# Second half of the heads weighed with high and low halves, in a fused cross-attention and mixture-of-experts kernel

## The reference

```
x = x + tanh(g_xattn) * xattn(layernorm(x), ctx)       # q @ Wq, ctx @ Wk, ctx @ Wv, softmax, @ Wo + bo
x = x + tanh(g_ffn) * (sum over 8 of 32 experts, weighted, + shared expert)(layernorm(x))
```

## Time and profile before

| | us |
|---|---|
| median of 3 runs | 660.29 (659.31 to 665.08) |
| profiled execution | 661.07 |
| its span | 658.9 |
| attention loop, 24 batches | about 61 to 310 |
| expert stage | from about 350 |

### The profile page before, as it was taken

How to read it: one execution, slowest core, us unless ns; L and a number is a source line. 1 busy time by engine, 2 the same in 40 slices (tenths; PEclk the granted TensorE clock), 3 DMA queues, 4 the chain that set the end, 5 groups by cost and what they waited for, 6 DMA issues and landing times.

```text
span 658.9 us, 13957 instructions
## 1 busy us (share of the span) xinstructions
PE 642.4 (97%) x3716; PEld 482.5 (73%) x3716; DVE 540.0 (82%) x1379; ACT 389.6 (59%) x738; POOL 344.7 (52%) x364
## 2 busy tenths in 40 slices
PE   8999999999999999999999999999999999999997
PEld 5666765767667676676658878788887878788785
DVE  6979978899898998989887969878695877869565
ACT  3565665666666665666556555555555555555553
POOL 4224645464544645546302656666565656657653
PEclk9999998999999999999999999999999999999999
DMA  8323222233323332223225844263645435364550
GB/s 185 101 65 82 80 71 61 79 78 79 80 63 80 80 78 80 62 84 84 59 68 142 184 109 129 73 163 81 163 113 128 131 73 140 86 159 113 139 137 16
DMA packets 63276, 65.58 MB, mean 100 GB/s; under 512 B 26112, under 2 KB 41600, under 8 KB 63232
## 3 DMA queue, kind: packets, MB, share of 16 engines
q1 hardware_dynamic: 63232, 65.07, 39.3%
HBM read 61.64 MB, written 2.88 MB: 98 GB/s over the span
## 4 chain that ended last, share of the span: by engine, by line
PE 68%; issue 9%; DVE 6%; ACT 5%; DMA 4%; POOL 4%; SPq 2%; DVEq 1%; ACTq 0%; POOLq 0%
PE bank L1220 13%; PE bank L1221 13%; PE bank L1222 13%; PE bank L1309 7%; PE bank L1333 5%; POOL halves L538 4%; DVE halves L820 3%; PE bank L1256 3%; PE bank L1276 3%; DMA sums<-wbc 2%; PE bank L1285 2%; PE bank L1279 2%; PE bank L1282 2%; DMA sums<-area 1%; SPq L311 1%
## 5 line engine op out<-in xcount | busy, mean ns | idle before, releaser
L538 POOL TENSOR_TENSOR halves<-area,halves 128x512 fp32r<-128x512 f32 x134 | 174.4, 1301 | 139.5 <-ACT halves L687 135.9
L700 ACT ACTIVATE area<-bank 128x512 f32<-128x512 f32 x136 | 81.4, 599 | 111.8 <-PE bank L1222 108.8
L625 ACT ACTIVATE area<-bank 128x512 f32<-128x512 f32 x128 | 69.5, 595 | 104.1 <-PE bank L1285 104.1
L1176 DVE TENSOR_TENSOR bank<-area,bank 128x512 f32<-128x512 f32 x128 | 88.7, 693 | 50.5 <-PE bank L1222 50.1
L1220 PE MATMUL bank<-x2t_hi,w_hi 128*128 128x512 f32 x272 | 110.3, 406 | 0.1
L1221 PE MATMUL bank<-x2t_hi,w_lo 128*128 128x512 f32 x272 | 107.2, 394 | 0.0
L1222 PE MATMUL bank<-x2t_lo,w_hi 128*128 128x512 f32 x272 | 106.4, 391 | 0.0
L472 POOL TENSOR_TENSOR ctx_hi<-ctx_raw,ones_col 128x128 fp32r<-128x128 f32 x32 | 27.4, 858 | 137.7 <-DMA ctx_raw<-ctx_t 137.7
L687 ACT ACTIVATE halves<-area 128x512 fp32r<-128x512 f32 x136 | 85.0, 626 | 17.1 <-DVE area L1187 16.7
L829 DVE TENSOR_REDUCE row_max<-bank 128x4 f32<-128x512 f32 x128 | 82.1, 684 | 6.1 <-PE bank L1256 3.4
L1187 DVE TENSOR_TENSOR area<-bank,wbc 128x512 f32<-128x512 f32 x128 | 86.5, 681 | 0.5 <-DMA wbc<-rows_dram 0.5
(11 more groups left out here) (149 smaller groups left out, 1261.7 us busy)
## 6 DMA issues: line engine op xcount, KB each, us to landing
wbc<-rows_dram SPq DMA_DIRECT2D x126, 256.0 KB, 4.2
inverse_bc<-inverse_dram SPq DMA_DIRECT2D x64, 256.0 KB, 3.5
w_raw<-experts SPq DMA_DIRECT2D x32, 102.0 KB, 2.0
ctx_raw<-ctx_t SPq DMA_DIRECT2D x32, 64.0 KB, 1.9
ctx_keys<-ctx_nat SPq DMA_DIRECT2D x32, 64.0 KB, 2.0
out<-area SPq DMA_DIRECT2D x7, 256.0 KB, 3.9
max_rows<-max_t SPq DMA_DIRECT2D x64, 4.0 KB
area<-wq_t SPq DMA_DIRECT2D x1, 512.0 KB, 4.7
```

What stands on the lines that cost most here:

```text
L538: nc.gpsimd.tensor_tensor(hid_lo[:, u % SLOTS, :], hid[:, u % HIDS, :], raw(hid_hi[:, u % SLOTS, :]), ALU.subtract).then_inc(hidlo_ready, 1)
L700: nc.scalar.activation(silu_g[:, u % 2, :], gate_ps[u % 2][:], ACT.Silu).then_inc(silu_ready, 1)
L1176: nc.vector.tensor_tensor(up_ps[u % UPS][:], silu_g[:, u % 2, :], up_ps[u % UPS][:], ALU.mult)\
```

## The change

From batch t = 3 on (LATE_FROM), and up to t = 27, the second half of the heads is weighed with halves too. `late_high` on ScalarE rounds the exponentials of groups 2 and 3 into the same `p_hi[q]` that the first half uses, once the first half's weighing has let it go. `late_low` on GpSimd makes the low halves, at the start of the next batch in its queue. `weigh_late` on TensorE takes the place of `weigh` for t - 1. As the buffers are shared, `probs_high` now waits for the late weighing of the batch before. Keys are split from t = 3 on.

Moved: `g_low` in odd b goes ahead of both scalings; `u_out(t, 0, 0)` goes behind `g_high` and `late_high`; `probs_high` always behind the two `u_out` of t - 1; `load_raw` on SyncE ahead of the maxima and the sums.

```diff
--- before.py
+++ after.py
@@ -68,7 +68,7 @@
 LN_AT = {0: range(0, 8), 1: range(8, RSTD_LEVELS)}
 AHEAD = 2
 STATS_AT = {2: (2,), 3: (3,), 4: (4,), 5: (5,), 6: (6, 7)}
-HALVED_FROM = CB
+HALVED_FROM, LATE_FROM = CB, CB - 1
 NB_SEAM = (NCH - 2) * CB
 SEAM = {4: (1, 6), 5: (6, 10), 6: (10, 14), 7: (14, 21)}
 LATE = {NB - 2: 3, NB - 1: 12}
@@ -208,6 +208,7 @@
         maxt_done, maxt_ready = sem("maxt_done"), sem("maxt_ready")
         st_done, exp_ready = sem("st_done"), sem("exp_ready")
         phi_ready, plo_ready = sem("phi_ready"), sem("plo_ready")
+        latehi_ready, latelo_ready = sem("latehi_ready"), sem("latelo_ready")
         keyshi_ready, keyslo_ready = sem("keyshi_ready"), sem("keyslo_ready")
         u_done, u_ready, inverse_ready = sem("u_done"), sem("u_ready"), sem("inverse_ready")
         norm_ready = [sem("norm_even_ready"), sem("norm_odd_ready")]
@@ -358,13 +359,13 @@
             def attention(c, first, last):
                 for b in range(CB):
                     t = CB * c + b
+                    if not last:
+                        wait_first(ctx_ready, t + 1)
+                        load_raw(b, (t + CB) * P)
                     if not (last and b == CB - 1):
                         load_max_row(t + 1, (b + 1) % 2, t - 1)
                     if not (first and b == 0):
                         spread_sums(t - 1, (b - 1) % CB)
-                    if not last:
-                        wait_first(ctx_ready, t + 1)
-                        load_raw(b, (t + CB) * P)
                     if not (last and b >= 2):
                         wait_first(wsplit_ready, t + 1)
                         load_weights(b % 2, (t + 2) * WSTEP)
@@ -481,9 +482,16 @@
                 wait(pool, u_done, 4 * (t - 2) + 4)
                 nc.gpsimd.tensor_tensor(keys_hi[:, b % 2, :], ctx_keys[:, b, :], ones_col[:].broadcast_to([P, 3 * CD]),
                                         ALU.mult).then_inc(keyshi_ready, 1)
-                pool.wait_ge(keyshi_ready, t + 1 - HALVED_FROM)
+                pool.wait_ge(keyshi_ready, t + 1 - LATE_FROM)
                 nc.gpsimd.tensor_tensor(keys_lo[:, b % 2, :], ctx_keys[:, b, :], raw(keys_hi[:, b % 2, :]), ALU.subtract)\
                     .then_inc(keyslo_ready, 1)
+
+            def late_low(t):
+
+                for q in range(2):
+                    pool.wait_ge(latehi_ready, 2 * (t - LATE_FROM) + q + 1)
+                    nc.gpsimd.tensor_tensor(p_lo[q], probs_t[:, 2 + q, :, :].rearrange("p h n -> p (h n)"),
+                                            raw(p_hi[q]), ALU.subtract).then_inc(latelo_ready, 1)
 
             def split_weights(slot, t, nth, contexts):
 
@@ -517,7 +525,9 @@
             def attention(c, first, last):
                 for b in range(CB):
                     t = CB * c + b
-                    if not first and not last:
+                    if not first and not (last and b > 0):
+                        late_low(t - 1)
+                    if not last and not (first and b < CB - 1):
                         split_keys(b, t, c)
                     split_weights(b % 2, t, 2 * c + b // 2, NB if last else t + CB)
                     add_bias(t, c)
@@ -628,10 +638,17 @@
             def probs_high(t):
 
                 act.wait_ge(exp_ready, 4 * t + 2)
-                wait(act, u_done, 4 * t - 2)
                 for q in range(2):
+                    act.wait_ge(u_done, 4 * (t - 1) + q + 3)
                     nc.scalar.activation(p_hi[q], probs_t[:, q, :, :].rearrange("p h n -> p (h n)"), ACT.Copy)\
                         .then_inc(phi_ready, 1)
+
+            def late_high(t, q):
+
+                act.wait_ge(exp_ready, 4 * t + q + 3)
+                act.wait_ge(u_done, 4 * t + q + 1)
+                nc.scalar.activation(p_hi[q], probs_t[:, 2 + q, :, :].rearrange("p h n -> p (h n)"), ACT.Copy)\
+                    .then_inc(latehi_ready, 1)
 
             def attention(c, first, last):
                 for b in range(CB):
@@ -641,15 +658,13 @@
                     exp_of(t, 0, 1)
                     if not (last and b == CB - 1):
                         max_out(t + 1, (b + 1) % 2, 2 * c + (b - 1) // 2 + 1)
-                    if not first and not last and b % 2 == 1:
+                    if not (first and b == 0):
+                        for q in range(2):
+                            u_out(t - 1, (b - 1) % CB, 1, q)
+                    if not first and not last:
                         probs_high(t)
                         if b == 1:
                             xt_high(c + 1)
-                    if not (first and b == 0):
-                        for q in range(2):
-                            u_out(t - 1, (b - 1) % CB, 1, q)
-                    if not first and not last and b % 2 == 0:
-                        probs_high(t)
                     if last and b == CB - 1:
                         x2t_out(1, scores_ps[1])
                     if first and b == 1:
@@ -661,9 +676,17 @@
                     exp_of(t, 1, 1)
                     if last and b == 1:
                         sigmoid_high(0, ut_ps)
+                    late = not last and not (first and b < CB - 1)
+                    if late:
+                        late_high(t, 0)
+                    if late and b % 2 == 1:
+                        g_high(2 * c + 2 + b // 2, b // 2)
+                        late_high(t, 1)
                     u_out(t, b, 0, 0)
-                    if b % 2 == 1 and not last:
-                        g_high(2 * c + 2 + b // 2, b // 2)
+                    if late and b % 2 == 0:
+                        late_high(t, 1)
+                    if first and b == 1:
+                        g_high(2, 0)
                     u_out(t, b, 0, 1)
                     if last and b == 0:
                         x2t_out(0, ut_ps)
@@ -834,7 +857,6 @@
 
                 for q in range(2):
                     dve.wait_ge(phi_ready, 2 * (t - HALVED_FROM) + q + 1)
-                    wait(dve, u_done, 4 * (t - 1) + q + 1)
                     nc.vector.tensor_tensor(p_lo[q], probs_t[:, q, :, :].rearrange("p h n -> p (h n)"),
                                             raw(p_hi[q]), ALU.subtract).then_inc(plo_ready, 1)
 
@@ -1050,6 +1072,8 @@
 
                         if h == 0 and not first:
                             batch_stats(t - CB, b)
+                        if h == 1 and b % 2 == 1 and first:
+                            g_low(2 * c + 2 + b // 2, b // 2)
                         if h == 1:
                             if first and b >= 2:
                                 normalise(t - 2, (b - 2) % CB, 0)
@@ -1062,8 +1086,6 @@
                         if first:
                             for n in STATS_AT.get(step_of_chunk, ()):
                                 chunk_stats(n)
-                        if h == 1 and b % 2 == 1 and first:
-                            g_low(2 * c + 2 + b // 2, b // 2)
                         if h == 1:
                             if not (first and b < 3):
                                 residual(t - 3)
@@ -1111,10 +1133,10 @@
                     batch_mean(t - CB, b)
                     if b == CB - 1:
                         keep_means(t - b - CB)
-                    normalise(t - 2, (b - 2) % CB, 0)
                     if b % 2 == 1:
                         g_low(2 * c + 2 + b // 2, b // 2)
-                    normalise(t - 2, (b - 2) % CB, 1)
+                    for q in range(2):
+                        normalise(t - 2, (b - 2) % CB, q)
 
             attention(0, True, False)
             with dve.Fori(1, NCH - 1) as c:
@@ -1288,7 +1310,7 @@
             def weigh_halves(t, b, q):
 
                 if q == 0:
-                    pe.wait_ge(keyslo_ready, t + 1 - HALVED_FROM)
+                    pe.wait_ge(keyslo_ready, t + 1 - LATE_FROM)
                 pe.wait_ge(phi_ready, 2 * (t - HALVED_FROM) + q + 1)
                 wait(pe, u_ready, 4 * (t - 1) + q + 3)
                 cols = slice(0, CD + 1) if q == 0 else slice(CD, 3 * CD)
@@ -1297,6 +1319,21 @@
                 nc.tensor.matmul(ps, keys_lo[:, b % 2, cols], p_hi[q], start=False, stop=False)
                 pe.wait_ge(plo_ready, 2 * (t - HALVED_FROM) + q + 1)
                 nc.tensor.matmul(ps, keys_hi[:, b % 2, cols], p_lo[q], start=False, stop=True).then_inc(u_done, 1)
+
+            def weigh_late(t, b):
+
+                pe.wait_ge(keyslo_ready, t + 1 - LATE_FROM)
+                cols = (slice(0, CD + 1), slice(CD, 3 * CD))
+                ps = (u_ps[0][0:CD + 1, :], u_ps[1][0:P, :])
+                for q in range(2):
+                    pe.wait_ge(latehi_ready, 2 * (t - LATE_FROM) + q + 1)
+                    pe.wait_ge(u_ready, 4 * t + q + 1)
+                    nc.tensor.matmul(ps[q], keys_hi[:, b % 2, cols[q]], p_hi[q], start=True, stop=False)
+                    nc.tensor.matmul(ps[q], keys_lo[:, b % 2, cols[q]], p_hi[q], start=False, stop=False)
+                for q in range(2):
```

(7 more changed lines are left out.)

## The result

| | before | after |
|---|---|---|
| median of 6 runs, us | 660.4 (659.3 to 665.1) | 691.9 (689.8 to 694.6) |
| ratio | | 1.046, 95% interval 1.043 to 1.050 |
| profiled execution, us | 661.1 | 693.7 |
| its span, us | 658.9 | 691.9 |
| loop, from the `scores` of batch 4 to those of batch 28, us | 61.00 to 309.89 = 248.9 | 60.82 to 340.00 = 279.2 |

The time is 0.9 us above the range of the forecast (657 to 691) and 12 above its point. The direction was right. Most of the loss is in the loop: +30.3 us of the +33.0 in the span.

What follows compares the result with a forecast made beforehand. TensorE was taken as the bound, VectorE close behind. Per pair −0.4 work, −0.3 wait, +0.75 and +1.65 gave +1.7 us; twelve pairs, 20.4 us, on 661.07 gave 681.5, as median 680.7, rounded to 680; range 657 to 691.

Steps and rivals of the forecast that it cites:

- The mechanism that made the forecast slower: VectorE's two-SBUF-input scalings and GpSimd's SBUF-reading subtractions exclude each other, so project_out waits; a pair gets 1.7 us longer.
- its two waits: TensorE at project_out waits 0.75 us in one tile of a pair and 1.65 us in the other.
- the wait for L820: TensorE's 0.3 us wait before the even tile's scores, for the queries' low halves, goes: 3.6 us saved over 12 pairs.
- TensorE's own work: Weighing two heads' groups with halves instead of fp32 saves 0.2 us a tile over 25 tiles, 5 us.
- the order in chunk 0 and the last chunk: Edits at the loop's two ends touch one tile each and cost under 1 us.
- Odd into even tile: From the even tile's scores, two scalings and one subtraction last 3.55 us; project_out, reached at +2.75, waits 0.75.
- The even tile: Two scalings and two subtractions meet from about +8.6, 4.7 us until +13.35; project_out, reached at +11.7, waits 1.65.
- The rest of the pair: After the second project_out starts, 9.1 us less the 0.3 us wait, 8.8, giving a pair of 22.15 us.
- SyncE's queue: With load_raw ahead, scaling's end to invert takes 5.65 us instead of 5.5; closes on 22.2 us a pair, late next.
- rival 3: SyncE's queue sets the pace as scaling delays return through inverse, maxima and sums: pairs 22.6 to 23.0, 687 to 692; 0.08.
- its only gain: Moving load_raw ahead ends the context's split at +7.4 to +7.9, out of the way of scalings and subtractions; no price.
- Rival 1: Subtractions early enough or running beside the scalings, so project_out finds its operands at +2.75: only savings stay, 652.5 us; 0.17.

Runs made afterwards that it cites:

- experiment 3: Changed kernel with both loop scalings replaced by a sum with one input in SBUF, scaling by inverse sums left out: 661.0 us, ratio 0.998 to the kernel before.
- 7b: Kernel before with only the low halves of the queries moved ahead of both scalings: 657.8 us, ratio 0.994.
- experiment 2: Changed kernel with each GpSimd subtraction replaced by two 16-column subtractions and two 496-column fills, similar time, almost no SBUF reading: 680.7 us, ratio 1.029.

## Why the prediction was right in direction and too small

The mechanism that made the forecast slower is the one that the runs show, and its two waits came out to 0.3 us. What failed is a step beside it, and terms put at nothing. In its own terms the forecast was +20.4 us; the span grew by 33.0. (The sum of 680.7 us also rounds to 681, not to 680.) Of the 12.6 between them 4.2 are in pairs at full clock (mainly the wait for L820, taken as gone), 5.7 in the long pairs of the loop (the clock, which has no term, and the first pair) and 2.7 outside the loop.

**TensorE's own work.** 0.2 us a tile. In the run of experiment 3, where nothing else interferes, scores to project_out fall from 2.96 to 2.67 (−0.29), but the stretch behind project_out grows from 2.38 to 2.45, twice a pair. A pair goes from 20.5 to 20.24: 0.13 us a tile, 3 us in all instead of 5. And that is eaten by the two ends of the loop.

**The two ends.** The prediction has "the order in chunk 0 and the last chunk" at under 1 us. The first pair is 24.59 in the run of experiment 3 against 20.55 before: the transpose of the maxima waits for VectorE's residual there, in the changed kernel's timeline of TensorE as in that run. Behind the loop TensorE waits for VectorE's normalised x, and the tile there is 2.5 us longer than before; in the kernel before that product has no such wait (L820 in this row is a line of after.py and not the L820 of the prediction):

```profile
64.41 0.38 PE L1288 MATMUL bank<-ident,row_max 128*16 128x128 f32 x1 [2.40 <-DVE x_sb L883]
...
349.56 0.66 PE L1249 MATMUL bank<-ident,xn 128*128 128x128 f32 x4 [1.60 <-DVE xn L820]
```

**The wait for L820.** Wrong, and this is the step of the sum whose mechanism failed: "L820 now starts when ScalarE's high halves come ... TensorE's 0.3 us wait goes: 12 pairs × 0.3 = 3.6 us". The stretch at whose end it lies did not shrink: 6.48 and 6.77 us instead of 6.36 and 6.75. VectorE works in order, and invert, ahead of it, waits 1.08 us for the sums in the pairs b = 2 and 3; I had priced load_raw's 0.6 us in that very queue and not carried it over. The saving was also too large by its own rows: L820's end moves from 166.43 to 166.25, which is 0.2 us and not 0.3. 7b, which has the move without load_raw's, shows it at 3.7 us in the median, with a clock that did not fall in its profiled execution.

**Odd into even tile.** Scalings and one subtraction in 3.55 us, project_out from +2.75 to +3.5. Measured 3.45, and +3.42 in the median. Right.

**The even tile.** Scores at +5.9 (measured +5.86), late_high(E, 0) ready at +8.7 (+8.7: the subtraction starts at 188.15, +8.8), invert at +9.15 (+8.85), four operations ending at +13.35 (+13.43), project_out there (+13.5). Right to 0.3 us, and experiment 3 shows the cause.

**The rest of the pair.** 8.8 us, from project_out of O to the next pair. Measured 8.9 and 9.2 in pairs at full clock (2.45 + 6.48 and 2.45 + 6.77): the 0.3 of L820 and 0.07. This is the pair of 22.55 instead of 22.15, some 4 to 5 us in all.

**What was missing.** The clock, for which the sum has no term. It fell in three project_outs and in the first pair, for 17.1 us in all instead of 3.4, which is worth at most 6.8 us; that the longer waits of TensorE bring this about is not shown, as other pairs have them at full clock. With the first pair, where two causes mix, the excess is 5.7 us more than before in the profiled execution. The profile before had two long pairs (103.26 to 107.86 for scores to project_out is one) that I had averaged into 20.74 a pair without asking what they were. In the three executions where the mean clock was 0.995 the changed kernel took 689.8 to 690.5 us, inside the range of the forecast.

**SyncE's queue.** I had it as a cost late next and in rival 3. load_raw's move has two signs: alone it costs 6 us, in the changed kernel it saves 20, as it takes the context's split out of the way of the scalings. The prediction has that in half a sentence ("its only gain") at no price.

**The rivals.** Rival 1's point of decision, that a scaling and a subtraction together last under 0.35 us more than the scaling, is what experiment 3 brings about, and the time is then 661, not 652.5. Rival 3's figures (687 to 692) hold the result, but not for its reason alone: its pairs of 22.6 to 23.0 are met by half of those at full clock (22.7), the others last 22.5, and the rest of the time lies at the clock and at the two ends.

## What to carry to other kernels

Before work is given to GpSimd, list the VectorE instructions with two inputs in SBUF that lie in the same stretch, and let both sets run one behind the other in the sum: an engine that is busy 53% of the time has no room if its work falls there. Ask for a moment, not for a total: which instructions have to be over before the bounding engine's next one, and how long they take in a row, on whichever engines. And a reordering is worth measuring alone; here one part of the change was a gain of 0.6% that the rest buried.

## What was not expected of the hardware

In experiment 2 a fill on GpSimd (496 columns, 0.51 us) does not hold up VectorE's scalings: they take 1.22 us, and the fills beside them 0.50 to 0.51. A subtraction of 16 columns, 0.22 us alone, can wait 0.9 us for one. So in these runs the exclusion goes by what GpSimd reads, and a small reader can wait about as long as a large one: 0.9 us for 16 columns, 0.8 to 1.0 for 512 (2.1 to 2.3 us instead of 1.3).
